# Turned weights ahead of keys and values in one attention, other steps, engines and fold places in two self attentions

## The chip, the cores and the metric

One Trainium2 chip, of which this kernel uses 1 core. The time is that of the device, in microseconds (us), from the start to the end of one execution. PE is TensorE (its weight loads are shown as PEld), DVE VectorE, ACT ScalarE, POOL GpSimd and SP SyncE, which only issues transfers here.

## The reference, cut to what matters

Two layers of a Perceiver, on 128 sequences of 32 tokens with 128 features, each sequence with a context of 257 rows:

```python
x = x + xattn0(ctx, layernorm(x))        # one head
x = x + attn0(layernorm(x))              # 16 heads, with relative positions
x = x + ffn0(layernorm(x))               # 8 experts, two for each token
x = x + xattn1(layernorm(x), ctx)        # 16 heads of 8 features
x = x + attn1(layernorm(x))              # 16 heads, 4 for keys and values, causal, rotary factor
x = x + ffn1(layernorm(x))               # 8 experts, two for each token

# xattn1:  q = x @ Wq.T ; k = ctx @ Wk.T ; v = ctx @ Wv.T
#          softmax(q k / sqrt(128)) v, then @ Wo.T + bo
# attn0:   softmax((q + u) k + shifted (q + v) p) val, then @ Wf + bf
# attn1:   x + (softmax over earlier tokens of q k / sqrt(8)) v @ w_o, on x / rms(x)
# ffn:     two best experts by logits; each: layernorm, fc1, gelu, fc2, times its gate
```

## The kernel before

Tokens lie in 32 tiles of 128, a tile being 4 sequences of 32 tokens. X stays in SBUF. The program is a row of passes with a barrier between them: setup, `cross_one_head`, `relative_scores`, relative attention (`self_attention` as "p4"), experts, `cross_many_heads` ("p6"), causal attention (`self_attention` as "p8"), experts, and a combining pass. The order of work on an engine is the order in which each engine's block is written. Nothing schedules it afterwards; engines meet at semaphores.

**Steps.** In the self attentions `each_step(STEPS, work)` draws `work(n, at)` for step n, fully unrolled. `at(k)` is the tile that is k steps behind (tile n − k), "live" if it exists. So a tile goes through the stages 0 to 5 in six steps, while each engine handles up to six tiles in a step. For a tile: z, the normalised X (DVE, L287, stage 0); zT, z turned by PE (L1191) and copied out by ACT (L1242 or L1245); q and k (PE L1163 and L1164, stage 1; ACT L1227 and L1228; DVE L1333); V (PE L1177, stage 2; ACT L1262 in four copies into `v_all`, two buffers); the scores (PE L1154, stage 3), DVE's sum with bias or mask (L1314) and maximum (L1320), POOL's subtraction (L1375), ACT's exponential (L1253); the turned weights pT (DVE L1327, stage 4), their product with V (PE L1211), o (DVE L1350 and L1352); oT (PE L1171, stage 5, ACT L1234), y (PE L1184), xb on POOL (L1386; in causal attention it takes zres, ACT L1271) and X (DVE L1341) with its statistics (L238 and L241). PE's scores wait for the newest X, because y lies in a bank that they write.

**Routing.** Behind the attention of a group of 4 tiles, `Routing` chooses the two experts of each token and its slot, in pieces spread over later steps: POOL's statistics (L264), ACT's rows (L875), PE's turning and logits (L800, L816), DVE's choice (L938 to L972), the ranks (PE L835 to L837, DVE L984 to L992), ACT's slots (L885), and then 16 scatters of POOL for each group, L776, that send rows to the experts' regions in memory. `READY` is the step in which a group's first piece is drawn, `AFTER` the number of steps behind the last tile, and the numbers in `group_at(n, lag)` place each piece. After the last step PE counts the tokens (`pe_count`, L847), DVE works out the table of jobs (`dve_table`, L1004 to L1049), and the pass ends when all scatters have landed.

**Folds.** Relative attention also folds the experts' layernorm into their weights, for the pass that follows: PE (L1202), ACT (L1277, eight of 128x512) and one sum of DVE (L1359), one expert in each of steps 36 to 43.

**Many heads.** `cross_many_heads` goes over the tiles by two in a loop (`over_tiles`), four sequences b in each. In a unit b, PE makes the scores of this sequence (L1495), keys and values of the sequence two ahead (L1503, L1505), the turned weights of the one before (L1516: ACT's p_prob turned into two halves of a bank, which ACT at L1608 and DVE at L1686 copy to p_pT), shares (L1536, L1537), a matmul on z, q or y by b, and the weighted sum of the one two before (L1545). DVE makes the maximum (L1634) and ACT four exponentials (L1592) and the copy of keys and values (L1601).

## Time and profile before

| | us |
|---|---|
| median of 3 runs | 1579.13 (1577.33 to 1583.44) |
| the profiled execution | 1578.75 |
| its span | 1576.9 |
| relative attention | 199.6 to 462.6 |
| many heads | 630 to 1160 |
| causal attention | 1160 to 1398 |

Busy shares of the span: PE 81%, PEld 70%, DVE 64%, ACT 53%, POOL 53%. The mean clock granted to TensorE is 0.894 of full speed. The page shows that no single engine fills the span, so what matters in a stretch is which wait ends last there. A row of a timeline gives the start, the duration, engine, line and operation; the bracket says how long the engine idled before it and what released it.

### The profile page before, as it was taken

To read this page: it belongs to the slowest core of one execution; us is meant where nothing else is said; L and a number is where in the kernel's file an instruction comes from. 1 tells how busy PE (TensorE), PEld (TensorE's weight loads), DVE (VectorE), ACT (ScalarE), POOL (GpSimd) and SP (SyncE) were. 2 spreads that over 40 slices of the span, in tenths; PEclk is the share of its full clock that TensorE was granted. 3 is DMA by queue.
4 is the path that set the end of the run, shared out by engine and by line. 5 is a ranking of instruction groups with operands and counts; after the bars stand their busy time and mean duration, and the time that the engine had idled before them with its cause. 6 is when DMAs were issued, how large, how long until landed. Compare 5 with 4: busy or idle time off the path is not lost. (4 is left out here: it accounts for less than half of the span.)

```text
span 1576.9 us, 48801 instructions
## 1 busy us (share of the span) xinstructions
PE 1274.6 (81%) x15330; PEld 1110.2 (70%) x15331; DVE 1008.2 (64%) x3247; ACT 842.2 (53%) x2658; POOL 834.0 (53%) x1700
## 2 busy tenths in 40 slices
PE   3777778989729996899999999999969877449991
PEld 2655777878729996677777777777758877349991
DVE  4655367877436664677777777777749878433334
ACT  1555356565314442577777777777737665224440
POOL 2555024666636564465665656565534566646661
PEclk9999578787559998899999999999969999569995
DMA  7998552121112221322111111111000000122215
GB/s 228 257 263 212 205 169 79 58 62 53 35 49 72 59 65 44 103 63 89 33 50 33 50 33 50 33 50 30 15 15 3 14 26 23 45 61 68 70 57 168
DMA packets 91997, 122.01 MB, mean 77 GB/s; under 512 B 12689, under 2 KB 67218, under 8 KB 91858
## 3 DMA queue, kind: packets, MB, share of 16 engines
q1 hardware_dynamic: 74194, 82.77, 17.8%
q0 software_dynamic: 12288, 34.82, 7.4%
q10 hardware_dynamic: 5376, 2.63, 0.6%
q8 instruction: 80, 1.31, 0.3%
q14 instruction: 59, 0.48, 0.1%
HBM read 89.68 MB, written 30.49 MB: 76 GB/s over the span
## 5 line engine op out<-in xcount | busy, mean ns | idle before, releaser
L1592 ACT ACTIVATE p_prob<-six,p_nm 128x257 f32<-128x257 f32 x512 | 236.4, 475 | 134.9 <-DVE p_nm L1634 134.9
L1634 DVE TENSOR_REDUCE p_nm<-six 128x2 f32<-128x514 f32 x256 | 165.1, 687 | 23.2 <-PE six L1495 21.3
L1842 PE MATMUL bank<-sb_w,m_experts_aT 128*128 x1152 | 155.7, 278 | 6.4 <-ACT m_experts_aT L1871 3.9
L1821 POOL DMA_INDIRECT expert_outputs<-m_experts_y,m_experts_dest x144 | 142.7, 991 | 26.0 <-POOL m_experts_tiny L1820 12.7
L1858 PE MATMUL six<-m_experts_xT,m_experts_w 128*128 128x128 f32 x1152 | 155.9, 279 | 0.0
L1842 PEld LDWEIGHTS bank<-sb_w,m_experts_aT 128*128 128x128 f32 x1152 | 140.2, 192 | 11.7 <-issue 11.2
L776 POOL DMA_INDIRECT expert_inputs<-p_r_x,p_r_slot x128 | 126.0, 984 | 41.2 <-issue 34.5
L1375 POOL TENSOR_TENSOR p_score<-p_score,p_mx 128x512 f32<-128x512 f32 x64 | 67.1, 1049 | 150.5 <-DVE p_mx L1320 148.7
L1858 PEld LDWEIGHTS six<-m_experts_xT,m_experts_w 128*128 128x128 f32 x1152 | 143.3, 196 | 0.6 <-issue 0.2
L1516 PE MATMUL six<-sb_const,p_prob 128*128 128x128 f32 x1024 | 132.8, 273 | 1.8 <-ACT p_pT L1608 1.5
L1495 PE MATMUL six<-p_kv,p_q_all 32*128 32x257 f32 x1024 | 93.2, 426 | 33.8 <-ACT p_prob L1592 33.6
L1516 PEld LDWEIGHTS six<-sb_const,p_prob 128*128 128x128 f32 x1024 | 116.0, 141 | 2.7 <-ACT p_prob L1592 1.8
L1686 DVE COPY p_pT<-six 128x512 f32<-128x512 f32 x128 | 87.3, 682 | 42.1 <-PE six L1516 42.1
L1592 ACT ACTIVATION_READ_ACCUMULATOR p_prob<-six,p_nm 128x1 f32 x512 | 104.0, 203 | 0.0
L1820 POOL TENSOR_TENSOR m_experts_tiny<-sb_const 128x1 f32<-128x1 f32 x144 | 39.6, 275 | 112.7 <-DVE m_experts_y L1899 61.2
L1735 POOL TENSOR_TENSOR p_spread<-p_recip,sb_const 128x128 f32<-128x128 f32 x128 | 51.3, 401 | 86.5 <-DVE p_recip L1682 86.3
L1503 PE MATMUL bank<-p_ctxT,sb_w_WkT_x 128*128 128x256 f32 x256 | 90.9, 437 | 0.8 <-ACT p_kv L1601 0.8
L1601 ACT ACTIVATE p_kv<-bank 128x512 f32<-128x512 f32 x128 | 78.0, 610 | 24.3 <-PE bank L1505 24.3
L1154 PE MATMUL six<-p_kT,p_q_all 32*128 32x32 f32 x2048 | 83.9, 285 | 5.9 <-issue 3.7
L1495 PEld LDWEIGHTS six<-p_kv,p_q_all 32*128 32x128 f32 x1024 | 44.1, 184 | 63.1 <-issue 63.1
L1871 ACT ACTIVATE m_experts_aT<-m_experts_h 128x512 f32<-128x512 f32 x72 | 45.5, 632 | 78.8 <-DVE m_experts_h L1916 45.6
L1262 ACT ACTIVATE p_v_all<-bank 32x128 f32<-32x128 f32 x256 | 71.0, 277 | 25.8 <-PE bank L1211 16.5
(287 smaller groups left out, 3472.0 us busy)
## 6 DMA issues: line engine op xcount, KB each, us to landing
ctxN_ring<-ctxN POOLq DMA_DIRECT2D x32, 516.0 KB, 10.4
ctxT_ring<-ctxT SPq DMA_DIRECT2D x32, 514.0 KB, 13.2
p_ctxT<-ctxT SPq DMA_DIRECT2D x32, 514.0 KB, 3.6
m_experts_x<-expert_inputs SPq DMA_DIRECT2D x144, 64.5 KB
bd_scores<-p_rows SPq DMA_DIRECT2D x32, 256.0 KB, 2.7
p_bd<-bd_scores SPq DMA_DIRECT2D x32, 256.0 KB
sb_w<-w SPq DMA_DIRECT2D x32, 256.0 KB
p_y<-expert_outputs SPq DMA_DIRECT2D x32, 128.0 KB, 3.3
```

Source lines behind the costliest of these rows:

```text
L776: m.nc.gpsimd.indirect_dma_start(m.xs_dram[:, :], bass.IndirectOffsetOnAxis(ap=self.slot[:, TOPK * t + k:TOPK * t + k + 1], axis=0), self. ...
L1154: last = mm(quad[:, g, keys], q_all[rows, t.par, b], kT[rows, t.par, keys], start=True, stop=True, tile_position=(32 * g, 0))
L1495: last = mm(scores_ps[:, g, 0:CTX], q_all[rows, t.par, b], kT[rows, t.par, b, :], start=True, stop=True, tile_position=(32 * g, 0))
L1503: mm(ps[6][:, 0:LAST], m.w["WkT_x"][:, :], ctxT[:, t.par, b, 0:LAST], start=True, stop=True)
L1516: last = nc.tensor.transpose(turned_ps[g // 2][:, g % 2, n * P:(n + 1) * P], prob[:, b, g, n * P:(n + 1) * P], ident)
L1592: last = nc.scalar.activation(prob[:, b, g, :], scores_ps[:, g, 0:CTX], ACT.Exp, bias=nm[:, b % 2, g:g + 1], accum_out=total[:, b % 2, g:g ...
L1601: nc.scalar.activation(kv[:, t.par, u, :].rearrange("p (k n) -> p k n", k=2)[:, :, 0:LAST], kv_ps, ACT.Copy).then_inc(s["kv"], 1)
L1634: nc.vector.tensor_reduce(nm[:, b % 2, g:g + 2], scores_ps[:, g:g + 2, 0:CTX], AX.X, ALU.max, negate=True).then_inc(s[most], 1)
L1686: nc.vector.tensor_copy(pT[:, u % 2, 2:4], turned_ps[1]).then_inc(s["pT_b"], 1)
L1821: nc.gpsimd.indirect_dma_start(m.ys_dram[:, :], bass.IndirectOffsetOnAxis(ap=dest[:, t.par:t.par + 1], axis=0), y[:, t.par, :], None).then ...
L1842: last = nc.tensor.matmul(ps[6 + t.two][:, 0:D], aT[:, t.two, f * P:(f + 1) * P], m.w2[:, DS(held[p] + f * D, D)], start=(f == 0), stop=(f ...
L1858: last = nc.tensor.matmul(ps[2 + t.two][:, f * P:(f + 1) * P], w[:, t.two, f * P:(f + 1) * P], xT[:, t.two, :], start=True, stop=True)
```

## The change

Three things, in three passes.

1. `cross_many_heads`: in each unit PE's turned weights of the unit before are drawn ahead of keys and values.
2. `self_attention`, both uses: z is made by ACT (Identity with scale RN and the bias `minus`, which POOL prepares at the start) as the first thing in a step. o stays in its place in the ring but is drawn at the start of the next step (stage 5); oT, y and X follow one step later (stage 6), xb at stage 5. PE's order in a step is oT, scores, q and k, [routing], zT, V, y. ACT's is z, [slots], oT, k and q2, zT, [turned], V, exponential, [rows], zres. `v_all` has three buffers. The routing's lags from the logits on grow by one, READY from 8 to 9, AFTER from 18 to 19.
3. Relative attention's folds are drawn in steps 46 to 53, behind the last rank, with four steps more.

```diff
-    READY = 8
-    AFTER = 18
+    READY = 9
+    AFTER = 19
...
-    STEPS = TILES + Routing.AFTER
+    STEPS = TILES + Routing.AFTER + (4 if relative else 0)
...
-    FOLDS = range(36, 36 + E)
+    FOLDS = range(TILES + 14, TILES + 14 + E)
...
-        v_all = sb("v_all", [P, 2, B4 * G, H4, HD + 1])
+        v_all = sb("v_all", [P, 3, B4 * G, H4, HD + 1])
...
+                t = at(6)
+                if t.live:
+                    pe.wait_ge(s["o"], t.nth())
+                    if at(1).live:
+                        pe.wait_ge(s["zT"], at(1).nth())
+                    routing.pe_turned_read(pe, n)
+                    nc.tensor.transpose(oT_ps, o[:, t.par, :], ident).then_inc(s["oT_ps"], 1)
                 t = at(3)
...
-                    if t.past(3):
-                        pe.wait_ge(tail.x_new, t.before(3))
+                    if t.past(4):
+                        pe.wait_ge(tail.x_new, t.before(4))
...
-                t = at(5)
-                if t.live:
-                    pe.wait_ge(s["o"], t.nth())
-                    if at(1).live:
-                        pe.wait_ge(s["zT"], at(1).nth())
-                    routing.pe_turned_read(pe, n)
-                    nc.tensor.transpose(oT_ps, o[:, t.par, :], ident).then_inc(s["oT_ps"], 1)
+                t = at(0)
+                if t.live and t.past():
+                    pe.wait_ge(s["zT"], t.before())
+                if at(6).live:
+                    pe.wait_ge(s["oT"], at(6).nth())
+                routing.pe_turn(pe, n)
+                if t.live:
+                    pe.wait_ge(s["z"], t.nth())
+                    nc.tensor.transpose(zT_ps, z[:, t.par, :], ident).then_inc(s["zT_ps"], 1)
                 t = at(2)
...
         @block.scalar
         def _(act):
             def work(n, at):
+                t = at(0)
+                if t.live:
+                    act.wait_ge(s["minus"], 2)
+                    if t.past(2):
+                        act.wait_ge(s["zT_ps"], t.before(2))
+                    nc.scalar.activation(z[:, t.par, :], m.X[:, t.cols()], ACT.Identity, scale=m.RN[:, t.cols(1)],
+                                         bias=minus[:, t.cols(1)]).then_inc(s["z"], 1)
                 routing.act_slots(act, n)
...
             def work(n, at):
-                t = at(0)
-                if t.live:
-                    if t.past(2):
-                        dve.wait_ge(s["zT_ps"], t.before(2))
-                    normed(m, z[:, t.par, :], t, m.RN).then_inc(s["z"], 1)
+                t = at(5)
+                if t.live:
+                    dve.wait_ge(s["o_ps"], t.nth())
...
+                routing.dve_logits(dve, n, at(5))
+                routing.dve_place(dve, n, at(5))
                 t = at(3)
...
+            minus_one = c[:, C_NEG:C_NEG + 1].broadcast_to([P, TILES])
+            nc.gpsimd.tensor_tensor(minus[:, :], m.MEAN[:, :], minus_one, ALU.mult).then_inc(s["minus"], 1)
+            pool.wait_ge(s["minus"], 1)
+            nc.gpsimd.tensor_tensor(minus[:, :], minus[:, :], m.RN[:, :], ALU.mult).then_inc(s["minus"], 1)
...
                     if cur.live:
                         scores(cur, b)
+                    t, u = near(at, b, -1)
+                    if t.live:
+                        turn_probs(t, u)
                     t, u = near(at, b, 2)
                     if t.live:
                         keys_and_values(t, u)
-                    t, u = near(at, b, -1)
-                    if t.live:
-                        turn_probs(t, u)
```

In what follows, lines of the changed kernel are 4 to 11 higher than before (nine from the many-heads pass on). PE in a unit of the many-heads loop with b=1 in front of one with b=2, before:

```order
L1495 MATMUL six<-p_kv,p_q_all 128x257 x4
L1503 MATMUL bank<-p_ctxT,sb_w_WkT_x 128x256
L1505 MATMUL bank<-sb_w_WvT_x,p_ctxT 128x128 x2
L1516 MATMUL six<-sb_const,p_prob 128x128 x8
L1536 MATMUL bank<-sb_const,p_spread 128x128
L1537 MATMUL bank<-sb_const,p_spread 128x32
L1569 MATMUL bank<-p_zT,sb_w_WqT_x 128x128
L1545 MATMUL bank<-p_pT,p_kv 32x128 x8
```

and in the changed kernel:

```order
L1504 MATMUL six<-p_kv,p_q_all 128x257 x4
L1525 MATMUL six<-sb_const,p_prob 128x128 x8
L1512 MATMUL bank<-p_ctxT,sb_w_WkT_x 128x256
L1514 MATMUL bank<-sb_w_WvT_x,p_ctxT 128x128 x2
L1545 MATMUL bank<-sb_const,p_spread 128x128
L1546 MATMUL bank<-sb_const,p_spread 128x32
L1578 MATMUL bank<-p_zT,sb_w_WqT_x 128x128
L1554 MATMUL bank<-p_pT,p_kv 32x128 x8
```

The eight transposes of p_prob now stand directly behind the scores, and the three matmuls of keys and values behind them. ACT in a step of relative attention with rows of routing, before:

```order
L1227 ACTIVATE p_kT<-six,sb_cols 128x128
L1228 ACTIVATE six<-six,sb_bqu 128x128
L1234 ACTIVATE p_oT<-six 128x128
L1242 ACTIVATE p_zT<-six,sb_cols 128x512
L1253 ACTIVATE p_prob<-p_score 128x512
L1262 ACTIVATE p_v_all<-bank 32x16x8 x4
L875 ACTIVATE p_r_x<-sb_X,p_r_negative,sb_RN 128x2x128 x2
```

and in the changed kernel:

```order
L1230 ACTIVATE p_z<-sb_X,p_minus,sb_RN 128x128
L1238 ACTIVATE p_oT<-six 128x128
L1244 ACTIVATE p_kT<-six,sb_cols 128x128
L1245 ACTIVATE six<-six,sb_bqu 128x128
L1253 ACTIVATE p_zT<-six,sb_cols 128x512
L1267 ACTIVATE p_v_all<-bank 32x16x8 x4
L1275 ACTIVATE p_prob<-p_score 128x512
L875 ACTIVATE p_r_x<-sb_X,p_r_negative,sb_RN 128x2x128 x2
```

z is new and first, oT stands ahead of k and q2, and the copies of V ahead of the exponential. PE at the end of relative attention, before (p_r_x and p_r_zT are routing's rows and their turned form, p_r_both, p_r_sums and p_r_carry the ranks', sb_ln_b with sb_w a fold):

```order
L837 MATMUL bank<-p_r_carry,sb_const 128x32
L816 MATMUL bank<-p_r_wg,p_r_zT 128x8 x2
L1202 MATMUL bank<-sb_ln_b,sb_w 128x1 x16
L835 MATMUL bank<-p_r_both,sb_const 128x32
L836 MATMUL bank<-p_r_sums,sb_const 128x32
L837 MATMUL bank<-p_r_carry,sb_const 128x32
L847 MATMUL six<-p_r_carry,sb_const 128x8
```

and in the changed kernel:

```order
L837 MATMUL bank<-p_r_carry,sb_const 128x32
L816 MATMUL bank<-p_r_wg,p_r_zT 128x8 x2
L835 MATMUL bank<-p_r_both,sb_const 128x32
L836 MATMUL bank<-p_r_sums,sb_const 128x32
L837 MATMUL bank<-p_r_carry,sb_const 128x32
L1206 MATMUL bank<-sb_ln_b,sb_w 128x1 x32
L847 MATMUL six<-p_r_carry,sb_const 128x8
```

All 32 matmuls of the folds now stand between the last rank and the count.

## Rows read from the trace of the kernel before

**Rows 1.** Timeline of PE, many heads: start us, us, engine, line, operation, [idle before].

```profile
834.82 0.72 PE L1495 MATMUL six<-p_kv,p_q_all 32*128 32x257 f32 x8 [0.31 <-ACT p_prob L1592]
...
836.45 1.04 PE L1516 MATMUL six<-sb_const,p_prob 128*128 128x128 f32 x8
...
838.54 0.72 PE L1495 MATMUL six<-p_kv,p_q_all 32*128 32x257 f32 x8
...
842.90 0.72 PE L1495 MATMUL six<-p_kv,p_q_all 32*128 32x257 f32 x8 [0.34 <-ACT p_prob L1592]
...
846.57 0.80 PE L1495 MATMUL six<-p_kv,p_q_all 32*128 32x257 f32 x8 [0.18 <-ACT p_prob L1592]
...
851.19 0.71 PE L1495 MATMUL six<-p_kv,p_q_all 32*128 32x257 f32 x8 [0.91 <-ACT p_prob L1592]
```

**Rows 2.** Timeline of ACT and DVE in the same units.

```profile
835.04 0.62 ACT L1608 ACTIVATE p_pT<-six 128x512 f32<-128x512 f32 x1
...
837.52 0.69 DVE L1686 COPY p_pT<-six 128x512 f32<-128x512 f32 x1 [0.55 <-PE six L1516]
...
840.02 1.28 DVE L1634 TENSOR_REDUCE p_nm<-six 128x2 f32<-128x514 f32 x2
```

**Rows 3.** Timeline of DVE and PE, relative attention, a step without routing.

```profile
226.51 0.27 DVE L1341 TENSOR_TENSOR sb_X<-six,p_xb 128x128 f32<-128x128 f32 x1
...
226.94 1.09 PE L1154 MATMUL six<-p_kT,p_q_all 32*128 32x32 f32 x32
...
227.73 0.34 DVE L287 TENSOR_SCALAR p_z<-sb_X,sb_MEAN,sb_RN 128x128 f32<-128x128 f32 x1
228.10 0.69 DVE L1314 TENSOR_TENSOR p_score<-six,p_bd 128x512 f32<-128x512 f32 x1
```

**Rows 4.** Window of four steps without routing: busy us of each engine, granted clock.

```profile
core 0: us, PE busy (x) PEld busy (x) DVE busy (x) ACT busy (x) POOL busy (x), PEclk, DMA share, GB/s
219.80:236.30 16.50, 16.20 (x321) 14.73 (x322) 15.73 (x48) 12.52 (x37) 6.35 (x11) 1.00 0.58 184
```

**Rows 5.** Timelines of ACT, POOL and DVE, causal attention, a step with scatters.

```profile
1305.26 0.49 ACT L1271 ACTIVATE p_zres<-sb_X,p_negative,sb_RZ 128x128 f32<-128x128 f32 x1
...
1305.32 0.96 POOL L776 DMA_INDIRECT expert_inputs<-p_r_x,p_r_slot  x1 [0.30 <-issue]
...
1305.84 0.47 DVE L287 TENSOR_SCALAR p_z<-sb_X,sb_MEAN,sb_RN 128x128 f32<-128x128 f32 x1
1307.02 0.69 DVE L1314 TENSOR_TENSOR p_score<-six,sb_const 128x512 f32<-128x512 f32 x1 [0.71 <-DMA sb_X<-x]
```

**Rows 6.** Timeline of DVE, causal attention, a step in which tokens are placed.

```profile
1288.10 0.35 DVE L287 TENSOR_SCALAR p_z<-sb_X,sb_MEAN,sb_RN 128x128 f32<-128x128 f32 x1
1288.35 0.69 DVE L1314 TENSOR_TENSOR p_score<-six,sb_const 128x512 f32<-128x512 f32 x1
```

**Rows 7.** Windows with DVE's score (L1314) alone: length, its busy us (count), granted clock.

```profile
283.10:390.90 107.80, 11.00 (x16) 0.79 0.20 61
1238.60:1336.50 97.90, 11.01 (x17) 0.98 0.08 24
```

**Rows 8.** Windows of all engines, as in rows 4, where the clock falls.

```profile
240.00:245.00 5.00, 2.54 (x30) 2.08 (x27) 3.47 (x6) 3.52 (x10) 2.89 (x5) 0.96 0.62 193
245.00:250.00 5.00, 5.00 (x72) 4.53 (x73) 2.27 (x10) 3.68 (x9) 0.00 (x0) 0.50 0.17 51
```

**Rows 9.** Timeline of DVE and PE in the first of these windows.

```profile
240.08 1.01 DVE L287 TENSOR_SCALAR p_z<-sb_X,sb_MEAN,sb_RN 128x128 f32<-128x128 f32 x1
...
242.81 1.16 PE L1177 MATMUL bank<-sb_w_Wv_a,p_zT 128*128 128x128 f32 x8 [1.68 <-ACT p_v_all L1262]
```

**Rows 10.** Timelines of PE, DVE and POOL at the end of relative attention.

```profile
423.69 6.96 PE L1202 MATMUL bank<-sb_ln_b,sb_w 128*128 128x1 f32 x32
...
440.44 0.19 DVE L984 TENSOR_TENSOR p_r_rank<-bank,sb_const 128x32 f32<-128x32 f32 x1 [12.48 <-remote]
...
442.50 0.96 POOL L776 DMA_INDIRECT expert_inputs<-p_r_x,p_r_slot  x1 [5.15 <-ACT p_r_slot L885]
...
452.38 0.96 POOL L776 DMA_INDIRECT expert_inputs<-p_r_x,p_r_slot  x1 [0.30 <-issue]
```

More of the change, by code:

```diff
@@ L770, in pool_scatter @@
         m, s = self.m, self.s
[L771 removed]
+        g, j = self.group_at(n, 10, self.GROUP)
         if g is not None:
@@ L880, in act_slots @@
         s = self.s
-        g, j = self.group_at(n, 9)
+        g, j = self.group_at(n, 10)
         if g is not None:
@@ L906, in dve_logits @@
         s = self.s
-        g, j = self.group_at(n, 4)
+        g, j = self.group_at(n, 5)
         if g is not None:
@@ L975, in dve_place @@
         s = self.s
-        g, j = self.group_at(n, 8)
+        g, j = self.group_at(n, 9)
         if g is None:
@@ L1247, in work @@
                 routing.act_turned(act, n, at(0))
+                t = at(2)
+                if t.live:
+                    act.wait_ge(s["v_ps"], t.nth())
+                    act.wait_ge(s["ones"], 4)
+                    if t.past(3):
+                        act.wait_ge(s["o_ps"], t.before(3))
+                    for h in range(H4):
+                        rows = slice(h * LEN, (h + 1) * LEN)
+                        nc.scalar.activation(v_all[rows, t.n % 3, :, h, 0:HD],
+                                             v_ps[rows, :].rearrange("p (n h d) -> p n h d", h=H4, d=HD)[:, :, h, :],
+                                             ACT.Copy).then_inc(s["v"], 1)
                 t = at(3)
@@ L1286, in _ @@
             dve.wait_ge(s["ones"], 1)
-            for par in range(2):
+            for par in range(3):
                 nc.vector.tensor_copy(v_all[:, par, :, :, HD], c[:, C_M4P:C_M4P + H4].unsqueeze(1).broadcast_to(
```

66 lines of the change are left out of this document (22 added, 44 removed).

## The prediction

> **What bounds the kernel now.** The profiled execution took 1578.75 us: a span of 1576.9 us and 1.85 us around it. The median of the runs shown is 1579.13 us, 0.4 us more, so I sum against 1578.75 and move the forecast by nothing. The change touches three passes of the span: relative attention (from 199.6 to 462.6 us), the attention over the context with many heads (630 to 1160 us) and causal attention (1160 to 1398 us). I read first the timelines of one regular stretch of each, then the last microseconds of relative attention.
>
> In the pass with many heads the time is a row of units, one for each of 4 sequences of 32 tiles. [rows 1] give PE's scores of five units: 3.72 us from b=1 to b=2, 4.36 to b=3, 3.67 to b=0 and 4.62 to the next b=1 (over the loop's branch; the tile in between without the branch takes less there). The first interval has no idle time in front of its scores: PE itself is the bound. The other three wait for ACT's exponentials, which wait for DVE's maximum.
>
> In the self attentions an unrouted step is a ring: DVE adds into X, PE's scores wait for that X, DVE's next score waits for PE. [rows 3]: X starts at 226.51, PE's scores at 226.94, the next DVE score at 228.10. DVE's z (0.34 us at 227.73) ends at 228.07, but PE's scores end only at 228.03, so z lies beside them. While routing scatters rows, another thing ends the step: [rows 5] show a scatter of POOL from 1305.32 to 1306.28, z ending at 1306.31, and the score only at 1307.02, 0.74 us after the scatter's end.
>
> **Turned weights before keys and values.** Nothing is added; PE's 8 transposes (L1516) and the three matmuls behind them trade places in 128 units. What changes is when the transposes can start. They write over the bank from which ACT copies the unit before, and that copy runs from 835.04 to 835.66 [rows 2], 0.84 us after the scores of 834.82 began. In the old place the transposes start at 836.45 [rows 1], so the copy has long ended. In the new place PE would be free for them about 0.7 us behind the start of the scores (their length, 0.72 us), and must wait until about 0.95: the copy's end and an estimate of 0.1 us for its signal (the copy's own follower in the rows, the exponential, gives no closer value). That is a hole of 0.25 to 0.3 us in PE.
>
> Its price by interval. From b=1 to b=2 PE is the bound: +0.3. From b=2 to b=3 the chain is share, masked and maximum on DVE; the maximum (840.02, [rows 2]) stands behind PE's end of the last unit, which moves with the start of the unit: 0. From b=3 to b=0 PE ends its unit just before the exponentials do: +0.08. In the tile with the branch the DVE copy that now waits 0.55 us for the transposes [rows 2] comes earlier, and the maximum behind it: up to −0.4. Two tiles together: 2×0.3 + 2×0.08 − 0.4 = +0.36. With some 15 pairs in the steady part: **+5 us**. Bounds: if the wait doesn't bind (the copy's signal comes with the last transposes of the bank and PE loses nothing), the two units in which DVE idles for 0.55 us give up to −0.4 us in a tile, 30×0.4 = −12; if each unit pays the hole where the exponentials follow PE, some 30×0.3 = +9 or +10.
>
> **Self attentions, steady.** DVE loses z (0.34 us in each of 64 tiles); ACT gets it. What ACT pays for such an operation is in [rows 5]: zres (L1271), the same form, takes 0.49 us. ACT is busy for 12.52 us in the four unrouted steps of [rows 4], 3.13 us a step, so with z 3.62 us in a step of 4.12. It fits, with half a microsecond for ACT's waits. Gain of the unrouted steps: 0, since z was beside PE's scores [rows 3].
>
> z counts where it is the last thing before the score: in the steps in which DVE chooses experts or places tokens but no second scatter runs. [rows 6]: z at 1288.10, score at 1288.35, with no idle time between. About 5 of the first routed steps and 5 placing steps in each pass are so, at 0.25 to 0.35 us: −3 for both passes. In the scatter steps the score waits beyond the scatter's end whatever DVE does [rows 5]: 0.
>
> Relative attention has one more loss. [rows 7]: 16 steps in 107.8 us, 6.74 us each, at a granted clock of 0.79, while causal attention makes 16 of its like in 97.9 us, 6.12 each, at 0.98. Before one fall of the clock PE was busy for 2.54 us of 5 at 0.96, then 0.50 [rows 8], that is 1.2 instead of 2.4 GHz. PE stood idle there for 1.68 us in front of the V matmuls, for ACT's copy of V [rows 9], which was queued behind an exponential that waited for POOL. The change puts the copy of V in front of the exponential, gives V a third buffer, and moves the turning of o to a full step after o was made. All three take PE's waits of this kind away. If relative attention reached causal attention's pace: 0.62×16 = −10 here, and about as much again at the start of routing at most, so −18 is the lower bound. If POOL's queue causes the idling some other way: 0. I take −8, about half of what 24 such steps would give (24×0.62 = 15), so **−11 for the steady parts** together with the −3.
>
> On a z of DVE beside POOL, the rows show 1.01 us at 240.08 instead of 0.34 while a subtraction of POOL runs [rows 9]. The Trainium skill (SBUF — State Buffer, two separate sides) says that DVE and GpSimd share a port pair, so that one of them is kept waiting. By that rule moving z to ACT would free POOL in each such overlap; from this row it is at most 0.7 us, seen once in a regular stretch, and I give it no term.
>
> **The end of relative attention.** [rows 10]: the folds of biases stand on PE in front of the last rank (32 of their matmuls run from 423.69 to 430.65), DVE reads that rank only at 440.44, and POOL's scatters pause for 5.15 us until 442.50. The last scatter ends at 453.34, the pass 9.2 us later. With the folds behind the rank, the slots of the last group can be there before the backlog runs dry: −5. Against it: each self attention has one step more before its last ranks, here some +1 to +2; and DVE's table of jobs now waits for the count behind the folds. The folds take 64×0.2175 = 13.9 us of PE (0.2175 from 6.96/32), so the table would end about when the scatters do. Also, DVE's 12.48 us are put down to "remote", PE having been done at about 432. If that comes from the scatters and not from the folds, it stays. I take **−3**, between −6 and +4. In causal attention the extra step costs 0 to 2: **+1**. The start of each pass gets a larger memset and two small POOL operations on one side, and z earlier on ACT on the other: 0, by estimate within 1.5.
>
> **Sum.** 5 − 11 − 3 + 1 = −8, and 1578.75 − 8 = **1571 us** (1570.75), 0.5% faster.
>
> **Rivals.**
> 1. *ACT becomes the bound of the self attentions and the hole in PE is real* (slower). ACT now serves z, oT, k, q2, zT, V and the exponential in this order. It decides from where its 3.62 us and its waits for PE pass the ring of 4.12 us, that is from 0.5 us of waiting on. Then some 14 steps of both passes get 0.3 us longer (+4), the exponential behind the copies of V holds up DVE's pT in 40 steps by 0.1 (+4), none of the −11 comes, and the pass with many heads pays +5 to +10: with −3 and +1 at the ends 1590 to 1595, or 1587 if half of it comes. For it: the exponential starts now as soon as POOL is done, and will stand behind 4 copies. Against: in the steps of 6 us ACT has room.
> 2. *The turned weights gain* (faster by more). The wait for ACT's copy doesn't bind, DVE's 0.55 us [rows 2] go: −12, with −8 to −13 of the rest: 1554 to 1559. Against it: the copy's end at 0.84 us is later than PE's readiness at 0.7.
> 3. *Nothing moves in the self attentions.* The scatter steps stay as they are, the clock falls as often, the stall of 12.48 us stays: −3 +5 +1: 1580 to 1583, no measurable change. For it: [rows 5] and the word "remote".
> 4. *The table ends last.* In relative attention the folds, the count and a table slowed by the scatters end behind the scatters: −3 becomes +4, the total 1578.
>
> **How the numbers follow.** A measurement of this kernel can tell 0.5% (7.9 us) from no change: 1571.2 and 1587.0 are the bounds. The forecast with its neighbourhood (1560 to 1577) has 0.45, rival 2 0.15, rivals 3 and 4 together 0.25, rival 1 0.15. The forecast stands on the lower bound, and its neighbourhood reaches further below than above (−18 for the clock against 0), so 0.30 of its 0.45 counts as faster. With rival 2 that makes faster 0.45, same 0.40, slower 0.15. The range 1553 to 1588 leaves out about 2 in 10: the far end of rivals 1 and 2.
>
> **What would show it.** In the pass with many heads: the interval from b=1 to b=2 at 4.0 (hole) or 3.7, the wait of the transposes for ACT's p_pT, and two tiles at 32.4 instead of 32.04. In relative attention: 16 scatter steps in 98 to 102 us and a granted clock above 0.9; if the clock still falls to 0.50, the step on PE's idling was wrong. V matmuls without a wait for ACT. In the drain: POOL's scatters without the pause of 5.15 us, and the count behind the folds not last. The forecast is wrong as a whole if ACT's z pushes k and q2 back in the unrouted steps (a period over 4.2 us), or if the hole in PE shows in every unit.

## The result and the profile after

The changed kernel is slower: a median of 1604.01 us over 4 runs (1600.24 to 1617.14) against 1578.53 us, a ratio of 1.0167 with a 95% interval of 1.0132 to 1.0203. The profiled execution took 1601.96 us with a span of 1600.2. The forecast was 1571 us, so both the sign and the size were wrong.

The three medians of the kernel before that stand beside the experiments are 1579.82 us (the first four), 1575.13 (the next four) and 1577.68 (the last four). So two kernels of different groups are compared by their ratios, and medians only within a group.

Divided at the same events in both kernels, the span goes like this (us; the events are the first and last DVE score of a self attention, PE's first matmul with the experts' own weights, L1842 before, and the first and last scores of the many-heads pass):

| stretch | before | after | difference | forecast |
|---|---|---|---|---|
| to the first score of relative attention | 212.0 | 213.6 | +1.6 | 0 |
| its 32 scores | 184.8 | 185.4 | +0.6 | about −9.5 |
| its last score to the experts | 72.6 | 80.7 | +8.1 | −3 |
| experts | 171.5 | 169.6 | −1.9 | |
| many heads | 504.6 | 502.2 | −2.4 | +5 |
| to the first score of causal attention | 26.8 | 24.9 | −1.9 | 0 |
| its 32 scores | 169.7 | 183.6 | +13.9 | about −1.5 |
| its last score to the end | 234.9 | 240.2 | +5.3 | +1 |

Each column is one profiled execution. Where the code of a stretch is the same in two kernels of this study, its length still differs: experts 168.0 to 172.7 us in the kernels with the changed self attentions; relative attention's scores 169.6 and 173.9 in one pair; causal attention's 183.6 and 186.9 in another, and 167.9 to 171.8 in three that have it as before. Below some 4 us a difference of one stretch says little by itself.

The largest piece, 13.9 us, is in causal attention. A step in which nothing is routed takes 4.87 us instead of 4.30, but there are only some five of these. Of its 31 intervals the first eight take 39.3 us instead of 35.9, the next eight, in which the routing starts, 51.4 instead of 42.5, and the last fifteen 92.8 instead of 91.3. So 9 us of the 13.9 lie in the second group. Timelines of ACT, PE and DVE of one unrouted step of the changed kernel (start us, us, engine, line, operation, [idle before]):

```profile
1206.02 0.48 ACT L1282 ACTIVATE p_zres<-sb_X,p_negative,sb_RZ 128x128 f32<-128x128 f32 x1
1206.40 0.48 ACT L1230 ACTIVATE p_z<-sb_X,p_minus,sb_RN 128x128 f32<-128x128 f32 x1
1206.91 0.28 ACT L1238 ACTIVATE p_oT<-six 128x128 f32<-128x128 f32 x1
1208.57 0.69 ACT L1256 ACTIVATE p_zT<-six,sb_cols 128x512 f32<-128x512 f32 x1 [1.39 <-PE bank L1186]
1209.16 1.17 ACT L1267 ACTIVATE p_v_all<-bank 32x128 f32<-32x128 f32 x4
1210.35 0.63 ACT L1275 ACTIVATE p_prob<-p_score 128x512 f32<-128x512 f32 x1
1210.88 0.48 ACT L1282 ACTIVATE p_zres<-sb_X,p_negative,sb_RZ 128x128 f32<-128x128 f32 x1
```

```profile
1207.28 0.30 PE L1180 MATMUL six<-sb_const,p_z 128*128 128x128 f32 x1 [0.68 <-ACT p_oT L1238]
1207.42 1.06 PE L1186 MATMUL bank<-sb_w_w_v,p_zT 128*128 128x128 f32 x8
...
1206.03 0.69 DVE L1333 TENSOR_TENSOR p_score<-six,sb_const 128x512 f32<-128x512 f32 x1 [0.73 <-PE six L1161]
...
1210.90 0.69 DVE L1333 TENSOR_TENSOR p_score<-six,sb_const 128x512 f32<-128x512 f32 x1 [0.73 <-PE six L1161]
```

Read in order they make a ring. ACT's oT (1206.91) lets PE turn z (1207.28, after an idle 0.68). The V matmuls stand behind that (1207.42 to 1208.48). ACT's copy of the turned z waits 1.39 us for them, since it writes the buffer that they read. Behind it come four copies of V, the exponential, zres, z, and again oT. ACT is busy for only 3.5 us of the 4.87, but the other 1.39 are a wait inside the ring. In [rows 3] the ring that set the step went through DVE and PE's scores.

When the routing starts, ACT's rows (L875) come into the same ring, and the clock falls. PE and ACT of the changed kernel in the longest of these steps, 9.72 us:

```profile
1224.33 0.66 PE L800 MATMUL six<-sb_const,p_r_x 128*128 128x128 f32 x2 [1.75 <-ACT p_oT L1238]
...
1224.99 1.92 PE L1186 MATMUL bank<-sb_w_w_v,p_zT 128*128 128x128 f32 x8
...
1227.01 0.69 ACT L1256 ACTIVATE p_zT<-six,sb_cols 128x512 f32<-128x512 f32 x1 [2.78 <-PE bank L1186]
```

and windows over the second group of eight intervals (length, busy us of PE, PEld, DVE, ACT and POOL, granted clock, DMA share, GB/s), before, changed, and in the kernel "V first" of the next section:

```profile
1208.20:1250.70 42.50, 37.67 (x673) 33.97 (x674) 37.92 (x135) 29.84 (x79) 20.36 (x31) 1.00 0.03 10
```

```profile
1215.80:1267.20 51.40, 43.61 (x674) 40.22 (x674) 35.85 (x122) 32.73 (x87) 15.33 (x26) 0.83 0.01 2
```

```profile
1194.90:1234.50 39.60, 36.27 (x674) 33.24 (x675) 35.18 (x122) 32.37 (x87) 15.33 (x26) 1.00 0.01 3
```

PE stands idle for 1.66 us and, one step on, 1.75 us in front of routing's rows, waiting for ACT's oT. Just before 1224 the granted clock falls to 0.50, PE having been busy for 5.80 of the 8.00 us from 1215 to 1223. The V matmuls then take 1.92 us instead of 1.06, and ACT, whose copy waits for them, idles for 2.78 us instead of 1.39. So the ring costs twice: by its own waits, and by a slower clock, which comes back with V first.

Relative attention has the same ring, 4.58 instead of 4.12 us an unrouted step. Its 32 scores take nearly the same time as before because something else got shorter there, as the experiments show.

In the many-heads pass, PE's scores and transposes, ACT's copy of the unit before, and DVE's copy of the other half:

```profile
843.18 0.72 PE L1504 MATMUL six<-p_kv,p_q_all 32*128 32x257 f32 x8
844.11 1.06 PE L1525 MATMUL six<-sb_const,p_prob 128*128 128x128 f32 x8 [0.21 <-issue]
847.12 0.72 PE L1504 MATMUL six<-p_kv,p_q_all 32*128 32x257 f32 x8
...
851.46 0.72 PE L1504 MATMUL six<-p_kv,p_q_all 32*128 32x257 f32 x8 [0.37 <-ACT p_prob L1601]
...
855.24 0.72 PE L1504 MATMUL six<-p_kv,p_q_all 32*128 32x257 f32 x8
...
859.11 0.71 PE L1504 MATMUL six<-p_kv,p_q_all 32*128 32x257 f32 x8 [0.16 <-ACT p_prob L1601]
```

```profile
843.39 0.62 ACT L1617 ACTIVATE p_pT<-six 128x512 f32<-128x512 f32 x1
...
845.27 0.67 DVE L1695 COPY p_pT<-six 128x512 f32<-128x512 f32 x1
```

The transposes start 0.93 us behind the start of the scores, 0.10 after the end of ACT's copy (844.01): the hole of the prediction. The interval from b=1 to b=2 is 3.94 us (3.72 in [rows 1]). But DVE's copy no longer waits, and the interval over the loop's branch falls from 4.62 to 3.87. Over two tiles of the steady part the sum is 31.70 instead of 32.04 us.

At the end of relative attention, PE's folds, ACT's folds, POOL's last scatter, the count and the table:

```profile
428.42 8.69 PE L1206 MATMUL bank<-sb_ln_b,sb_w 128*128 128x1 f32 x40 [0.28 <-issue]
...
440.13 0.16 PE L1206 MATMUL bank<-sb_ln_b,sb_w 128*128 128x1 f32 x1 [1.04 <-issue]
441.54 0.16 PE L1206 MATMUL bank<-sb_ln_b,sb_w 128*128 128x1 f32 x1 [1.25 <-issue]
442.94 0.16 PE L1206 MATMUL bank<-sb_ln_b,sb_w 128*128 128x1 f32 x1 [1.23 <-issue]
...
458.32 0.57 PE L847 MATMUL six<-p_r_carry,sb_const 128*128 128x8 f32 x2
```

```profile
447.84 0.72 ACT L1288 ACTIVATE sb_w<-sb_w,sb_ln_w 128x512 f32<-128x512 f32 x1 [11.22 <-remote]
...
450.44 0.96 POOL L776 DMA_INDIRECT expert_inputs<-p_r_x,p_r_slot  x1 [0.30 <-issue]
...
470.94 0.22 DVE L1049 TENSOR_TENSOR sb_gates<-sb_gates,p_r_moved 128x64 f32<-128x64 f32 x1
```

The scatters now run without the pause of [rows 10] and the last one starts at 450.44 instead of 452.38. The folds run at their pace for 8.69 us, then one at a time, 1.4 us apart and more, until shortly after the scatters end. The count comes at 458.32 and the table ends at 471.16, in place of 454.09 before. The table is the last work of the pass, 20 us behind the last scatter.

### The profile page after: what moved, and what is told of

Same layout as the page of the kernel before. It is cut to its first block and busy times, and to the rows that moved or that the text cites. A ratio compares the mean times of both kernels' runs of the same rounds, so it can differ in the third digit from the quotient of the medians.

```text
span 1600.2 us, 48893 instructions
## 1 busy us (share of the span) xinstructions
PE 1282.8 (80%) x15330; PEld 1116.8 (70%) x15331; DVE 982.0 (61%) x3185; ACT 861.4 (54%) x2722; POOL 831.8 (52%) x1704
## 5 line engine op out<-in xcount | busy, mean ns | idle before, releaser
L1525 PEld LDWEIGHTS six<-sb_const,p_prob 128*128 128x128 f32 x1024 | 110.2, 141 | 67.4 <-issue 59.6
L1525 PE MATMUL six<-sb_const,p_prob 128*128 128x128 f32 x1024 | 137.9, 278 | 20.0 <-issue 17.3
L1504 PE MATMUL six<-p_kv,p_q_all 32*128 32x257 f32 x1024 | 92.7, 429 | 14.8 <-ACT p_prob L1601 13.8
L1628 DVE COPY p_share<-bank 128x128 f32<-128x128 f32 x128 | 37.3, 292 | 93.7 <-PE bank L1554 93.7
L1880 ACT ACTIVATE m_experts_aT<-m_experts_h 128x512 f32<-128x512 f32 x72 | 45.4, 630 | 76.6 <-DVE m_experts_h L1925 40.4
L1514 PEld LDWEIGHTS bank<-sb_w_WvT_x,p_ctxT 128*128 128x128 f32 x512 | 78.7, 194 | 7.3
L1161 PEld LDWEIGHTS six<-p_kT,p_q_all 32*128 32x128 f32 x2048 | 74.2, 201 | 12.4 <-issue 5.6
```

The lines of the kernel that those rows point to most:

```text
L1161: last = mm(quad[:, g, keys], q_all[rows, t.par, b], kT[rows, t.par, keys], start=True, stop=True, tile_position=(32 * g, 0))
L1504: last = mm(scores_ps[:, g, 0:CTX], q_all[rows, t.par, b], kT[rows, t.par, b, :], start=True, stop=True, tile_position=(32 * g, 0))
L1514: last = mm(ps[6][:, LAST + n * P:LAST + (n + 1) * P], ctxT[:, t.par, b, n * P:(n + 1) * P], m.w["WvT_x"][:, :], start=True, stop=True)
L1525: last = nc.tensor.transpose(turned_ps[g // 2][:, g % 2, n * P:(n + 1) * P], prob[:, b, g, n * P:(n + 1) * P], ident)
```

## The experiments

All in one table first, in us. "Ratio" is to the kernel before, with its 95% interval; the other columns are stretches of the profiled execution, divided at the events named above: relative attention's scores, its drain (from its last score to the experts), many heads, causal attention's scores. A unit of 0.001 in a ratio is 1.6 us.

| kernel | ratio | scores, relative | drain | many heads | scores, causal |
|---|---|---|---|---|---|
| before | 1 | 184.8 | 72.6 | 504.6 | 169.7 |
| changed | 1.0167 (1.0132 to 1.0203) | 185.4 | 80.7 | 502.2 | 183.6 |
| V first | 0.9945 (0.9910 to 0.9979) | 173.5 | 80.8 | 501.3 | 167.0 |
| exponential first | 1.0203 (1.0150 to 1.0256) | 194.9 | 83.0 | 502.0 | 184.1 |
| z on DVE | 1.0029 (1.0003 to 1.0056) | 177.3 | 84.3 | 502.9 | 168.8 |
| folds back | 1.0075 (1.0049 to 1.0100) | 186.2 | 75.0 | 501.4 | 186.9 |
| before, with the turned weights' place only | 1.0003 (0.9987 to 1.0020) | 181.6 | 74.1 | 501.9 | 171.7 |
| before, with the folds' place only | 1.0061 (1.0034 to 1.0087) | 182.3 | 79.4 | 505.3 | 167.9 |
| V first, folds back | 0.9947 (0.9914 to 0.9981) | 169.4 | 75.4 | 502.6 | 163.7 |
| and oT behind q and k ("mended") | 0.9891 (0.9851 to 0.9931) | 169.6 | 73.3 | 502.4 | 159.0 |
| mended, z on DVE | 0.9901 (0.9862 to 0.9939) | 169.5 | 78.1 | 502.4 | 163.2 |
| mended, exponential first | 0.9963 (0.9939 to 0.9988) | 185.5 | 75.6 | 502.5 | 162.4 |
| before, with V's copies and third buffer only | 0.9914 (0.9876 to 0.9952) | 178.3 | 69.7 | 504.4 | 164.6 |
| mended, turned weights in the old place | 0.9902 (0.9865 to 0.9938) | 173.9 | 76.6 | 504.4 | 158.9 |

**V first.** The changed kernel, with the V matmuls ahead of the turned z on PE:

```diff
+                t = at(2)
+                if t.live:
+                    if t.past():
+                        pe.wait_ge(s["v"], t.before(1, H4))
+                    for b in range(B4):
+                        last = mm(v_ps[:, b * D:(b + 1) * D], zT4[:, t.par, b], wv, start=True, stop=True)
+                    last.then_inc(s["v_ps"], 1)
                 t = at(0)
...
                     nc.tensor.transpose(zT_ps, z[:, t.par, :], ident).then_inc(s["zT_ps"], 1)
-                t = at(2)
-                if t.live:
-                    if t.past():
-                        pe.wait_ge(s["v"], t.before(1, H4))
-                    for b in range(B4):
-                        last = mm(v_ps[:, b * D:(b + 1) * D], zT4[:, t.par, b], wv, start=True, stop=True)
-                    last.then_inc(s["v_ps"], 1)
```

> The changed kernel, with the V matmuls of a step back ahead of the turned z on PE (in both self attentions). Theory A (a ring through ACT and PE: the V matmuls stand behind the turned z, this one behind ACT's oT and z, ACT's copy of the turned z behind the V matmuls, the exponential behind the copies of V, and the next z behind the exponential): the V matmuls start at 0.5 us of a step instead of 1.39, the unrouted steps of causal attention go from 4.87 to 4.3 or 4.4 us and those of relative attention from 4.58 to 4.1 or 4.2, and the kernel takes 8 to 14 us less than the changed one: about 1590 to 1595. Theory B (ACT simply has too much to do with z in it): the steps stay within 0.1 us of 4.87 and 4.58, the kernel stays at 1602 to 1604. Theory C (the exponential is late because it stands behind the copies of V): as theory B, no more than 2 us less.

Measured: 1572.97 us, 31 below the changed kernel by the medians, 35 by the ratios. PE in an unrouted step of causal attention:

```profile
1181.95 0.39 PE L1171 MATMUL six<-p_zT,sb_w_w_k 128*128 128x128 f32 x2
1182.17 1.06 PE L1177 MATMUL bank<-sb_w_w_v,p_zT 128*128 128x128 f32 x8
1183.07 0.27 PE L1187 MATMUL six<-sb_const,p_z 128*128 128x128 f32 x1
...
1184.72 0.33 PE L1149 MATMUL six<-sb_const,p_o 128*128 128x128 f32 x1
1184.98 1.09 PE L1161 MATMUL six<-p_kT,p_q_all 32*128 32x32 f32 x32
```

The V matmuls stand directly behind q and k, and the turned z no longer waits. The step is 4.38 us, as theory A said; theories B and C fall. The whole gain is far more than the 8 to 14 us expected: 16.6 us in causal attention, 11.9 in relative attention, where the unrouted steps are only 0.2 us shorter. In causal attention 11.8 us of it come from the eight intervals in which the routing starts, 39.6 us at a granted clock of 1.00 in place of 51.4 at 0.83. The ring held routed steps up too, and the fall of the clock there goes with it.

**Exponential first.** The changed kernel, with the exponential ahead of the copies of V, as it was before:

```diff
+                t = at(3)
+                if t.live:
+                    act.wait_ge(s["shifted"], t.nth())
+                    if t.past(2):
+                        act.wait_ge(s["pT"], t.before(2))
+                    nc.scalar.activation(prob[:, t.par, :], score[:, t.par, :], ACT.Exp, scale=scale).then_inc(s["probs"], 1)
                 t = at(2)
                 if t.live:
                     act.wait_ge(s["v_ps"], t.nth())
...
-                t = at(3)
-                if t.live:
-                    act.wait_ge(s["shifted"], t.nth())
-                    if t.past(2):
-                        act.wait_ge(s["pT"], t.before(2))
-                    nc.scalar.activation(prob[:, t.par, :], score[:, t.par, :], ACT.Exp, scale=scale).then_inc(s["probs"], 1)
```

> The changed kernel, with ACT's exponential back ahead of the copies of V. Theory A: the same operations lie in the ring in another order, so the step stays at 4.87 and 4.58 us where nothing is routed, and the kernel at 1600 to 1606. Theory B: the same. Theory C: the exponential comes 1.2 us earlier in a step, the steps fall by up to 0.5 us, the kernel to about 1590.

Measured: 1613.92 us. Unrouted steps are unchanged (4.88 in causal, 4.45 to 4.73 in relative attention), so the order inside the ring doesn't matter, as theory A said. Theory C falls: no gain, but a loss, 9.5 us in relative attention's scores. No theory had said that, and the time lies above the 1600 to 1606 of theory A. It shows that the copies of V ahead of the exponential are a gain of this change there.

**z on DVE.** The changed kernel, with z back on DVE ahead of the score:

```diff
                 routing.dve_place(dve, n, at(5))
+                t = at(0)
+                if t.live:
+                    if t.past(2):
+                        dve.wait_ge(s["zT_ps"], t.before(2))
+                    normed(m, z[:, t.par, :], t, m.RN).then_inc(s["z"], 1)
```

> The changed kernel, with z back on DVE as the last thing before the score. Theory A: z's 0.49 us leave the ring, so the unrouted step goes from 4.87 to about 4.4 us (and 4.58 to 4.1 or 4.2), while in routed steps DVE pays 0.3 us again: 1592 to 1600. Theory B: the same 0.5 us, so this run does not part A from B, it prices z. If z were not in any ring, the time would stay or rise by 2 us.

Measured: 1586.03 us, 18 below the changed kernel by the medians (22 by the ratios), where 4 to 12 were expected (14.8 us come in causal, 8.1 in relative attention). z's 0.49 us on ACT cost that much only because they lie in the ring: see the same edit on the mended kernel below.

**Folds back.** The changed kernel, with the folds in steps 36 to 43 again:

```diff
-    STEPS = TILES + Routing.AFTER + (4 if relative else 0)
+    STEPS = TILES + Routing.AFTER
...
-    FOLDS = range(TILES + 14, TILES + 14 + E)
+    FOLDS = range(36, 36 + E)
```

> The changed kernel, with the folds of biases back in steps 36 to 43 and without the four added steps. Theory D (behind the last rank PE's folds run one instruction at a time beside the scatters, and the count and DVE's table, which wait for them, end the pass): relative attention's end comes 8 to 12 us earlier, the kernel at 1592 to 1595. Rival (the longer end of the pass comes from the step added to the routing and from late slots, not from the folds): 1600 to 1604.

Measured: 1593.48 us. The drain is 75.0 us instead of 80.7, and the table ends at 445.3 instead of 471.2. Theory D holds for the drain in sign, with 5.7 us instead of 8 to 12. The times differ by 10.5 (by the ratios 14.5, give or take 7), and the rest isn't in this stretch of the two profiled executions.

**Two parts alone, on the kernel before.** The turned weights' place only, and the folds' place only (in steps 45 to 52, since the last rank is in step 44 there):

```diff
                         scores(cur, b)
+                    t, u = near(at, b, -1)
+                    if t.live:
+                        turn_probs(t, u)
                     t, u = near(at, b, 2)
                     if t.live:
                         keys_and_values(t, u)
-                    t, u = near(at, b, -1)
-                    if t.live:
-                        turn_probs(t, u)
```

> The kernel before, with only the turned weights ahead of keys and values. Theory (as in the changed kernel's trace, where the many-heads pass from first to last scores is 502 us instead of 504): about 2.3 us less than before, 1576 to 1578, with b=1 to b=2 at 3.93 instead of 3.72 us and the loop's branch interval at 3.88 instead of 4.62. The prediction's own term for this part was +5. A gain of 12 would be its rival.

Measured: 1576.53 us, a ratio of 1.0003: no change that can be told. Its many-heads pass takes 501.9 us. All kernels with the turned weights ahead have 501.3 to 502.9 there, the four without 504.4 to 505.3. So the part brings 2 to 3 us in its pass; the whole time, between −2 and +3 us, doesn't show it. The prediction's +5 is out, as is the rival's −12.

```diff
-    STEPS = TILES + Routing.AFTER
+    STEPS = TILES + Routing.AFTER + (4 if relative else 0)
...
-    FOLDS = range(36, 36 + E)
+    FOLDS = range(TILES + 13, TILES + 13 + E)
```

> The kernel before, with only the folds of biases moved behind the last rank (steps 45 to 52, four steps more). Theory D (PE's folds are issued one by one at 1.4 us while the scatters run, and count and table wait for them): relative attention's drain gets 6 to 10 us longer, 1585 to 1589. The prediction said 2 to 5 us less: 1574 to 1577.

Measured: 1585.27 us, ratio 1.0061, and the drain 79.4 instead of 72.6 us. Theory D holds (6.8 us in the drain, 10 in the time), the prediction's term has the wrong sign. PE and ACT at the folds there:

```profile
427.53 9.55 PE L1202 MATMUL bank<-sb_ln_b,sb_w 128*128 128x1 f32 x44 [0.28 <-issue]
...
440.52 0.16 PE L1202 MATMUL bank<-sb_ln_b,sb_w 128*128 128x1 f32 x1 [1.26 <-issue]
...
441.24 0.72 ACT L1277 ACTIVATE sb_w<-sb_w,sb_ln_w 128x512 f32<-128x512 f32 x1 [8.43 <-remote]
441.93 0.16 PE L1202 MATMUL bank<-sb_ln_b,sb_w 128*128 128x1 f32 x1 [1.24 <-issue]
```

Again some 44 folds run at full pace and the next ones about 1.4 us apart, so this isn't bound to the changed order of steps.

**Both mends.** The edits of "V first" and of "folds back" together, in the changed kernel.

> The changed kernel with both mends: the V matmuls ahead of the turned z, and the folds in steps 36 to 43. If the two losses are independent, their gains add: 31 and 10 us below the changed kernel, 1560 to 1565. If the folds' loss depends on where the scatters meet them, 1566 to 1573.

Measured: 1564.17 us, a number within the first branch, but the kernel before ran 4.7 us faster in this group than in the first. By the ratios this kernel (0.9947) is no better than V first alone (0.9945), where adding the two gains would have given about 0.985. So it isn't shown that the gains add. What the profile does show is the folds' share of the drain, in three pairs: 5.4 us here (80.8 against 75.4), 5.7 with the ring in place and 6.8 on the kernel before.

**oT behind q and k.** Besides, PE's turning of o behind q and k, and ACT's oT behind k and q2:

```diff
-                t = at(6)
-                if t.live:
-                    pe.wait_ge(s["o"], t.nth())
...
-                    nc.tensor.transpose(oT_ps, o[:, t.par, :], ident).then_inc(s["oT_ps"], 1)
                 t = at(3)
...
                     mm(k_ps, wk, zT4[:, t.par, :, 0, :], start=True, stop=True).then_inc(s["qk_ps"], 1)
+                t = at(6)
+                if t.live:
+                    pe.wait_ge(s["o"], t.nth())
...
+                    nc.tensor.transpose(oT_ps, o[:, t.par, :], ident).then_inc(s["oT_ps"], 1)
                 t = at(2)
```

> As the run with both mends, and besides the turning of o goes back behind q and k on PE (and oT behind k and q2 on ACT). Theory: with V first the unrouted steps stand at 4.38 us because the turning of o (0.27 us) lies between the weighted sum and the scores on PE; without it they go to 4.12 in relative and 4.30 in causal attention, the kernel 1 to 4 us below the run with both mends. Rival: the z on ACT holds the ring (oT then comes 0.3 us later), and the steps stay at 4.38 or rise.

Measured: 1556.12 us, ratio 0.9891: the lowest of the study, 8 us below both mends where 1 to 4 were expected. PE in an unrouted step:

```profile
1175.97 0.27 PE L1171 MATMUL six<-sb_const,p_o 128*128 128x128 f32 x1
1176.08 1.06 PE L1177 MATMUL bank<-sb_w_w_v,p_zT 128*128 128x128 f32 x8
...
1177.68 0.90 PE L1215 MATMUL bank<-p_v_all,p_pT 128*32 128x36 f32 x32 [0.21 <-issue]
1178.70 1.09 PE L1154 MATMUL six<-p_kT,p_q_all 32*128 32x32 f32 x32
```

The scores start where DVE's X lets them, with nothing between them and the weighted sum. The steps are 4.30 and 4.12 us, the values of the kernel before and of the expectation. This is 0.26 us for about five steps of relative attention and less in causal attention, so most of the 8 us must lie elsewhere; it wasn't found where.

**z on DVE in the mended kernel.**

> The version with all three mends (V first, folds back, oT behind q and k; 1556 us), with z back on DVE. Theory (the prediction's: z lay beside PE's scores in unrouted steps, cost 0.25 to 0.35 us in some 10 steps of each pass in routed ones): 3 to 6 us more than with z on ACT, 1559 to 1562, unrouted steps unchanged at 4.12 and 4.30. Rival (z on ACT costs more than it brings): 1550 to 1555.

The edit is that of "z on DVE" above. Measured: 1560.39 us. Relative attention's scores are the same (169.5 against 169.6), causal attention's 4.1 us longer. Between the two the ratios differ by 0.001, with intervals of 0.004, so the time alone doesn't tell them apart; the profile says 0 and 4 us, where the prediction had 3 for both passes together, and 4 us is about what equal code differs by.

**Exponential first in the mended kernel.**

> The version with all three mends, with ACT's exponential back ahead of the copies of V. Theory (the copies of V behind an exponential that waits for POOL are what idles PE in relative attention and lets its clock fall): relative attention's 31 steps go from 170 us to 178 to 185, the clock granted in it falls, causal attention by 0 to 3 more: 1564 to 1572. Rival (the gain came from oT a step later): no more than 2 us slower.

The edit is that of "exponential first". Measured: 1569.31 us, 13 above the mended kernel by the medians, 11 by the ratios. Relative attention's scores go from 169.6 to 185.5 us, just above the expectation, causal attention's by 3.3. Windows over relative attention's scores: first the kernel before, then the mended one, then this one.

```profile
212.00:397.00 185.00, 165.43 (x2538) 151.56 (x2536) 147.19 (x462) 113.28 (x314) 103.96 (x165) 0.85 0.26 80
```

```profile
212.00:382.00 170.00, 143.84 (x2528) 132.99 (x2527) 134.65 (x423) 122.97 (x340) 97.76 (x156) 0.94 0.30 90
```

```profile
212.00:397.50 185.50, 158.58 (x2527) 146.20 (x2526) 134.04 (x423) 123.50 (x340) 98.60 (x159) 0.86 0.27 81
```

With the copies of V ahead, the clock granted in this stretch is 0.94 and PE's work takes 144 us; with the exponential ahead, 0.86 and 159 us for the same matmuls. The mended kernel with the turned weights in the old place, whose self attentions are those of the mended kernel, has 173.9 us at 0.89. So the order of the two blocks is worth 12 to 16 us here, by which of the two it is held against.

**Copies of V alone, on the kernel before.**

```diff
-        v_all = sb("v_all", [P, 2, B4 * G, H4, HD + 1])
+        v_all = sb("v_all", [P, 3, B4 * G, H4, HD + 1])
...
-                t = at(3)
-                if t.live:
-                    act.wait_ge(s["shifted"], t.nth())
...
                 t = at(2)
                 if t.live:
                     act.wait_ge(s["v_ps"], t.nth())
-                    act.wait_ge(s["ones"], 3)
-                    if t.past(2):
-                        act.wait_ge(s["o_ps"], t.before(2))
+                    act.wait_ge(s["ones"], 4)
+                    if t.past(3):
+                        act.wait_ge(s["o_ps"], t.before(3))
...
+                t = at(3)
+                if t.live:
+                    act.wait_ge(s["shifted"], t.nth())
...
```

> The kernel before, with only the copies of V ahead of the exponential on ACT and a third buffer of V. If the copies of V alone are the cause: relative attention 8 to 12 us shorter, 1565 to 1570. If they need oT, o and z out of the way too: 1574 to 1580. In unrouted steps the exponential comes 1 us later in a ring with room: no change there.

Measured: 1560.54 us, ratio 0.9914. This part alone makes the kernel 14 us faster (0.86%), in relative attention's scores (−6.5), its drain (−2.9) and causal attention's scores (−5.1). The time is below the expected 1565 to 1570, while the stretch of relative attention gives less than the expected 8 to 12; its granted clock goes from 0.85 to 0.89. It is most of what the mended kernel gains with all the others: the intervals of 0.9914 and 0.9891 overlap, so no run shows that the rest of the change brings anything.

**The mended kernel with the turned weights in their old place.**

> The version with all three mends, without the turned weights ahead of keys and values. From the trace of the changed kernel the many-heads pass gets 2.3 us longer: 1557 to 1560. From the run with this part alone (ratio 1.0003 with 0.17% on either side) the same to 1 us. More than 5 us would mean that the part works otherwise than the traces show.

The edit is that of the turned weights, undone. Measured: 1559.56 us, and 504.4 us of many heads instead of 502.4: the same 2 us.

## Why the prediction was wrong

**The step that failed is "It fits, with half a microsecond for ACT's waits".** It compared ACT's busy time, 3.13 + 0.49 us [rows 4, 5], with the length of a step. Busy time in the changed step is close to that (3.5 us). But the reordering drew PE's turned z behind ACT's oT and the V matmuls behind the turned z, while ACT's copy of the turned z overwrites what the V matmuls read. So ACT waits 1.39 us in the middle of its own chain, and where routing comes into that chain, 2.78 us. The prediction's own sign of being wrong, a period over 4.2 us in the unrouted steps, came: 4.58 and 4.87. Swapping two blocks on PE took the wait away and 31 to 35 us with it. The prediction named the order of ACT and the order of PE, and didn't follow the waits from one to the other and back. Rival 1 had the right pass and the right sign, and its point of decision (0.5 us of waiting) is what was passed; but it put the price at +8 and had the time at 1590 to 1595, with a chance of 0.15.

**Unrouted steps, 0:** measured +0.57 us a step in causal and +0.46 in relative attention. In the mended order it is 0, so what was said of z ([rows 3], beside PE's scores) was right. But these steps are only some ten in all, about 5 us. The greater part of the ring's cost lies in the routed steps that the prediction counted as a gain: +8.9 us in the eight intervals of causal attention, at a clock of 0.83 instead of 1.00.

**z in routed steps, −3:** in the mended kernel −4 in causal attention and 0 in relative attention. That agrees with the term, but the runs can't confirm it: the ratios differ by 0.001, and equal code differs by as much as the 4 us.

**The copies of V, with the third buffer and the later oT, −8:** the mechanism was right. Order and third buffer alone took 6.5 us off relative attention's scores; taking the order out of the mended kernel costs 12 to 16 us there, the clock falling from 0.94 or 0.89 to 0.86. The mended kernel's scores are 169.6 (or 173.9) us instead of 184.8, so the full gain lies between the −8 taken and the lower bound of −18. In the changed kernel the ring took all of it back: 185.4 us.

**The drain, −3:** measured +8.1. The scatters did lose their pause of 5.15 us [rows 10], as forecast, and rival 4 came, at twice its price. It was priced at +4 by the folds' own length (13.9 us), but they took 30 us, from 428.42 to 458.46, because eleven of them came 0.7 to 2.8 us apart. The table's 12 us came behind that. The folds' place makes 5.4 to 6.8 us of the drain; the rest is the later routing or the difference between executions.

**Turned weights, +5:** measured −2.4 in the pass. The hole was there and had its forecast size (transposes at 0.93 us; b=1 to b=2 +0.22 instead of +0.3), but the interval over the branch fell by 0.75 instead of 0.4, and the same interval of the tile without the branch, which had no term, by 0.1. Two tiles together came to −0.34 us where the sum had +0.36. DVE's copy no longer waits for the transposes, and over the branch DVE's maximum now starts 1.07 us behind PE's scores instead of 1.82 (846.57 to 848.39 before, 855.24 to 856.31 after).

**The last drain, +1:** +5.3, of which 4.8 us lie ahead of the experts. In the kernels with the shifted stages causal attention's last score to the last expert matmul takes 200 to 205 us, in those without 198 to 200. So the routing's later pieces seem to cost more than the 0 to 2 us that was put for one step; which piece it is wasn't tried.

**Left open.** The start and the experts' passes moved by +1.6 and −1.9 us, which is less than they differ by in equal code. And why folds come one by one beside the scatters: below.

## What to carry to other kernels

When a reordering moves work between engines, walk the ring: from one engine's instruction through its wait to the other engine and back to the same instruction one step later, buffers that are overwritten included. A comparison of busy time with the step's length doesn't see a wait that lies inside such a ring, and the mend can be a swap of two blocks (here the V matmuls ahead of the turned z, 31 to 35 us). Try each part of a composite change alone: one of the parts here was worth 14 us by itself, and two others hid it.

## What the runs showed of the hardware that was not expected

While POOL issued scatters back to back, every 1.26 us, PE, ACT and DVE, with work to do and nothing to wait for, issued instructions only at about 1.4 us after a stretch at full pace. PE's folds did so in the changed kernel after 40 at full pace, and in the kernel with the folds' place only after 44; ACT's next fold came after an idle of 11.22 us that the profile puts down to "remote". The full pace came back some 5 us after the start of the last scatter (folds from 455.53 with the last scatter at 450.44; from 451.75 with it at 447.09). DVE's table shows the same in the last drain, and did so in the kernel before already:

```profile
1377.62 0.23 DVE L1025 TENSOR_TENSOR p_r_before<-p_r_before,p_r_jobs 128x64 f32<-128x64 f32 x1 [1.21 <-DVE p_r_before L1024]
1379.01 0.22 DVE L1026 TENSOR_REDUCE p_r_first<-p_r_before 128x8 f32<-128x64 f32 x1 [1.16 <-issue]
1380.42 0.17 DVE L1027 TENSOR_SCALAR p_r_first<-p_r_first 128x8 f32<-128x8 f32 x1 [1.19 <-issue]
```

Its instructions from L1019 to L1041 take 22.2 us there (23.5 in the changed kernel) and 9.1 us in relative attention's drain of the kernel before, where they also run beside scatters, but behind the pause of 5.15 us [rows 10]. So a reader of the trace before could have seen the price of work placed beside a long run of scatters.

The cause isn't shown. That the first 40 or so run freely and the rest don't suggests that instructions run out rather than that an engine is slowed. The Trainium skill (Runtime: NRT & Kernel Launch, Instruction fetch mechanics) says that each engine's sequencer fetches its instructions by DMA in blocks into a first-in-first-out buffer. A fetch held up by the scatters' transfers would fit with that. The page also calls such fetches mostly hidden; in these rows, if it is the fetch, it isn't. Against it: from 425 to 456 us the trace of the changed kernel has no transfer of the kind "instruction", only the scatters' own, which take 14.5% of the DMA engines' time.

The granted clock followed the order of blocks, on PE itself and on another engine. Over the eight intervals in which causal attention's routing starts, it was 0.83, 0.83 and 0.96 in the three kernels with z on ACT and the turned z ahead of the V matmuls, and 1.00 in the eleven others. Over relative attention's scores it was 0.94 and 0.89 in two kernels with the mended self attentions, and 0.86 with the exponential ahead of the copies of V on ACT; before it was 0.85, and with the copies of V ahead 0.89. Over relative attention equal code differs by up to 0.05, so the second reading is weaker than the first.
